# Two transformer layers after an attention stage: where ScalarE writes the scaled and shifted layer norm input, between the squares and the copies of transposed weights

## The reference

```python
x = layernorm(x + split_attention(dynamic_conv(x)))          # x: 16 x 256 x 128, "stage a"
x = layernorm(x + two_layers(x))

def layer(x):                                                # twice, 8 heads of 64
    h = shift_token(x)
    q, k, v = split(h @ wqkv)
    q, k = rotary_xpos(l2norm(q) * qs, l2norm(k) * ksc)
    o = local_attention(q, k, v)                             # windows of 64, softmax over 128 keys
    x = x + o @ wo
    h = shift_token(x)
    h = (h - mean(h)) / sqrt(var(h) + 1e-5) * ln_g + ln_b
    a, g = split(h @ w1 + b1)                                # 341 columns each
    return x + (a * gelu(g)) @ w2 + b2
```

## Time and profile before

| | us |
|---|---|
| median of 3 runs (1402.93 to 1405.08) | 1403.01 |
| the profiled execution's own time | 1405.44 |
| its span, first to last instruction | 1403.6 |
| busy in it: PE | 1249.5 (89%) |
| busy: VectorE | 1231.8 (88%) |
| busy: ScalarE | 944.8 (67%) |
| busy: GpSimd | 943.0 (67%) |

### The profile page before, as it was taken

One profiled execution on the slowest core, in us unless ns is written; L12 is line 12 of the kernel. 1 busy time (PEld: TensorE's weight loads), 2 busy tenths in 40 slices (PEclk: granted clock), 3 DMA queues, 4 the chain that ended last, 5 costly groups with the idle time before them and its releaser, 6 DMA issues.

```text
span 1403.6 us, 36296 instructions
## 1 busy us (share of the span) xinstructions
PE 1249.5 (89%) x12288; PEld 977.4 (70%) x12288; DVE 1231.8 (88%) x2418; ACT 944.8 (67%) x1708; POOL 943.0 (67%) x915
## 2 busy tenths in 40 slices
PE   4799889898988988988788999999999999999986
PEld 3577667776767766766566777777777777677764
DVE  4899999999999999998488888988888888888873
ACT  3566565666665656664367888888888877778772
POOL 0734443444344334444799999999999999999971
PEclk9899999999999999998999999999999999999998
DMA  5000000000000000000111212111122122211110
GB/s 170 1 10 13 9 7 12 12 11 9 11 11 4 9 11 11 8 7 14 25 41 36 51 43 47 45 45 43 46 53 49 42 52 48 50 46 44 47 35 27
DMA packets 87052, 44.15 MB, mean 31 GB/s; under 512 B 43908, under 2 KB 80176, under 8 KB 86960
## 3 DMA queue, kind: packets, MB, share of 16 engines
q1 hardware_dynamic: 86960, 42.95, 12.3%
HBM read 19.86 MB, written 6.29 MB: 19 GB/s over the span
## 4 chain that ended last, share of the span: by engine, by line
DVE 36%; POOL 25%; issue 17%; PE 17%; SPq 2%; ACT 1%; DVEq 1%; POOLq 0%; DMA 0%; ACTq 0%
DVE sums L993 9%; POOL rnorm L660 9%; POOL kT L649 7%; DVE probs L1025 7%; DVE mx L1019 5%; POOL probs L710 3%; POOL kT L663 3%; PE bank L1399 2%; DVE xo L1054 2%; PE bank L1378 2%; PE bank L1360 2%; PE bank L1434 2%; SPq L476 1%; DVE conv L936 1%; PE bank L1462 1%
## 5 line engine op out<-in xcount | busy, mean ns | idle before, releaser
L625 POOL TENSOR_TENSOR probs<-probs,coef 128x1024 f32<-128x1024 f32 x128 | 239.6, 1903 | 201.2 <-DVE coef L985 201.2
L660 POOL TENSOR_TENSOR rnorm<-norm,halves 128x8 f32<-128x8 f32 x128 | 213.8, 1671 | 10.7
L785 ACT ACTIVATE probs<-probs 128x1024 f32<-128x1024 f32 x128 | 134.7, 1052 | 101.7 <-DVE probs L1025 101.2
L1280 PE MATMUL bank<-ident,probs 128*128 128x128 f32 x1024 | 143.1, 284 | 50.0 <-POOL probs L625 49.9
L772 ACT ACTIVATE wT<-bank 128x512 f32<-128x512 f32 x256 | 138.8, 596 | 63.6 <-PE bank L1280 62.4
L1019 DVE TENSOR_REDUCE mx<-bank 128x8 f32<-128x512 f32 x256 | 163.7, 680 | 14.7 <-PE bank L1293 13.3
L649 POOL TENSOR_TENSOR kT<-qT 128x512 f32<-128x512 f32 x128 | 163.8, 1280 | 8.4 <-DVE qT L1073 8.4
L1280 PEld LDWEIGHTS bank<-ident,probs 128*128 128x128 f32 x1024 | 115.4, 144 | 69.5 <-POOL probs L625 58.5
L1025 DVE TENSOR_TENSOR probs<-bank,mx 128x512 f32<-128x512 f32 x256 | 163.4, 679 | 0.0
L1293 PE MATMUL bank<-kT,qT 64*128 64x256 f32 x1024 | 154.7, 423 | 6.3 <-DVE probs L1025 6.3
L1319 PE MATMUL bank<-wT,v 128*64 128x128 f32 x2048 | 144.3, 284 | 11.0 <-DVE gate L931 6.2
(11 more groups left out here) (120 smaller groups left out, 3082.7 us busy)
## 6 DMA issues: line engine op xcount, KB each, us to landing
probs<-f_v SPq DMA_DIRECT2D x96, 128.0 KB, 2.3
res<-stage_x SPq DMA_DIRECT2D x48, 128.0 KB, 3.9
xn<-in_x SPq DMA_DIRECT2D x16, 128.0 KB, 2.2
xr<-in_x SPq DMA_DIRECT2D x16, 128.0 KB, 2.2
stage_x<-xo SPq DMA_DIRECT2D x32, 64.0 KB, 1.6
hn<-stage_x SPq DMA_DIRECT2D x32, 64.0 KB
mn<-mid SPq DMA_DIRECT2D x64, 32.0 KB
stage_x<-yo SPq DMA_DIRECT2D x16, 128.0 KB, 2.1
```

The lines of the kernel that those rows point to most:

```text
L625: nc.gpsimd.tensor_tensor(out=e[:, :, :, :], in0=e[:, :, :, :], in1=coef[r][:, 2, A_REP * ng:A_REP * (ng + 1), :].unsqueeze(3).broadcast_t ...
L660: nc.gpsimd.tensor_tensor(out=rnorm[:, at], in0=norm2[:, 1, at], in1=halves[:, 0:F_HEADS], op=ALU.pow).then_inc(rnorm_set, 1)
L785: nc.scalar.activation(e[:, :, :, :], e[:, :, :, :], ACT.Exp).then_inc(exp_done, 1)
L1280: ins = nc.tensor.transpose(banks[4 + hp][:, P * (2 * kb + hh):P * (2 * kb + hh + 1)], e[:, 2 * hh + hp, 2 * kb:2 * kb + 2, :], ident[:, :])
```

## The change

In each tile 0 step of the two layers ScalarE did `hidden_input` first, then the squares of the even block, then the two copies into `eT`, then the exponential. Now `hidden_input` stands behind the two copies and ahead of the exponential. Nothing is added or removed.

```diff
--- before.py
+++ after.py
@@ -876,9 +876,6 @@
                         late = n - F_ATT_LAG
                         if tile == 1 and prepares(turn, p, 2):
                             rounded(it, p + 2, turn)
-                        local = f_late(turn, s, "gates")
-                        if local is not None:
-                            hidden_input(it, local, layer_of(local))
                         if prepares(turn, p):
                             squares(4 * (unit + 1) + 2 * tile, 4 * (p + 1) + 2 * tile, 2 * tile, turn)
                         if f_exists(turn, s, F_ATT_LAG):
@@ -887,6 +884,9 @@
                                 wait(act, f_o_made, late)
                                 nc.scalar.activation(eT[:, 4 * k:4 * k + 4, :], banks[4 + k][:, :].rearrange("p (h q) -> p h q", h=4),
                                                      ACT.Copy).then_inc(eT_read, 1)
+                        local = f_late(turn, s, "gates")
+                        if local is not None:
+                            hidden_input(it, local, layer_of(local))
                         if f_exists(turn, s):
                             e = fE[s % F_RING]
                             act.wait_ge(f_sub, n + 1)
```

## The result

The changed kernel takes 1412.24 us (median of 4 runs, 1410.79 to 1413.52) against 1402.97 us for the kernel before in the same session (1402.14 to 1405.08). The ratio is 1.0064, with a 95% interval of 1.0048 to 1.0080: the change makes the kernel 9.3 us slower. 1412.0 was predicted.

What follows compares the result with a forecast made beforehand. Two rings of equal length, GpSimd's and PE with VectorE's, were taken to bound layer one. Layer one's 9.2 us less 0.4, layer two nothing, took the median from 1403.0 to 1411.8, said as 1412.0; range 1405.8 to 1415.5.

Steps and rivals of the forecast that it cites:

- L855's new place, and PE's wait: Layer one, tile 0: L855 ends at 1003.93, so PE's odd block loads 0.68 to 0.69 us later.
- The ring of 20.60 us: Layer one: PE and VectorE's chain from one `mT` to the next, at most about 0.1 us of slack against 20.68.
- Squares and copies gain nothing: ScalarE, tile 0: the squares could start 0.03 us earlier; the copies gain nothing, bounds 0 to 0.03 us.
- The exponential has cover: ScalarE, tile 0: it moves from 1003.37 to about 1003.84 at no cost, with 0.67 us of cover before VectorE's sum.
- GpSimd falls in behind: Layer one: VectorE's rotated blocks come late, so from the second unit on GpSimd waits too.
- Sum for layer one: A unit takes 21.29 us; 15 units take 319.35 us in place of 310.17, 9.2 us more, or 8.8 net.
- GpSimd's lead: Layer one: VectorE's rotation ends 1.15 us (tile 1) or 0.85 us (tile 0) before L649; swallows about 0.4 us once.
- Layer two: Odd block 0.61 us late, but units stay at 22.28 us; cost nothing, cover about 1.0 us a unit.
- GpSimd covers it: Rival: busy GpSimd sets the pace, so a delay on PE and ScalarE costs nothing; 1403.0 us, chance 0.11.
- Half covered: Rival: PE's 0.40 us of idleness a unit in layer one absorbs part of the delay; 1407.4 us, chance 0.11.
- Faster: Rival: PE's odd block does not wait, squares and copies come up to 0.14 us earlier; 1401.5 us, chance 0.05.
- Layer two as well: Rival: 15 further units in layer two pay 0.61 us each, 9.2 us; 1421 us, chance 0.04.

Runs made afterwards that it cites:

- GpSimd relieved: Kernel before, with GpSimd dividing four of eight heads in a step and not five, ScalarE one more: 1397.17 us, ratio 0.9963.
- the same three matmuls: Kernel before plus three extra 128x512 PE matmuls: ahead of tile 0's odd block 1412.16 us, or ahead of tile 1's v block 1403.60 us.

## Why the prediction was right, point by point

- **L855's new place, and PE's wait.** Right. L855 starts 2.62 us behind `mT` (2.65 predicted). The odd block loads 0.62 us later, and 0.68 to 0.69 was predicted: the way from the end of L855 to PE's load is 1011.75 - (1011.12 + 0.58) = 0.05 us and not the 0.10 of the earlier trace rows, the start is 0.03 us early, and L855 takes 0.58 and not 0.56 us.
- **The ring of 20.60 us.** Right, and it carried the forecast. 21.24 - 0.62 = 20.62, and with GpSimd relieved the old order runs at 20.59.
- **Squares and copies gain nothing.** Right (0.01 us).
- **The exponential has cover.** Right here: VectorE's sum of it starts at 1013.36 behind other work, as foreseen. But in the kernels in which PE does not wait for L855, the late exponential or late copies show a price of 0.11 to 0.15 us a unit through the copy of transposed q and k, a path that the prediction did not look at. In the changed kernel the odd block and all behind it come 0.62 us later, and the stretch shows no wait of PE for that copy; so that it costs nothing there is an outcome that I had not argued for.
- **GpSimd falls in behind.** Right in substance, partly wrong in place. I had it waiting ahead of L649 in tile 1, 0.6 us a unit. From the second unit on it waits at both places: ahead of tile 0's L649, 0.29 us in the unit shown, and ahead of tile 1's, 0.11 to 0.19 us. The view above counts 22 of these waits, 5.1 us.
- **Sum for layer one.** 318.53 - 310.17 = 8.4 us, against 9.2 predicted, or 8.8 with the 0.4 us that GpSimd's lead was to give back. That term was wrong: the lead was used up, but the units take 21.21 us from the first of the stretch on, so it made none of them shorter. GpSimd's lead does not lie on the ring that sets the pace. With the measured 0.62 us the sum is 15 x 21.22 = 318.3 us, against 318.53 found. The upper bound of 0.80 us a unit was not net of slack either: 0.79 - 0.08 is 0.71. What was given back came later, 0.65 us on the way into layer two: the lateness of `mT` against before is 1.5 us at the start of the stretch (1.15 of it from before the change acts), 9.8 at its end, 10.0 two units on and 9.35 where the second stretch begins.
- **Layer two.** Right: PE's waits for L710 shrink by what the wait for L855 adds, the unit takes 22.32 against 22.28 us, and the change there alone is not to be told from no change.
- **The total.** 1412.0 was said and 1412.24 measured. That it came out to 0.3 us is luck: a step of 9.0 us was forecast, the interval of the measured one reaches from 6.7 to 11.2 us, and the terms had errors of 1 us (the wait) and 0.4 us (the lead) that partly cancel. What was right is the mechanism and its size to within 1 us or so. The span of the profiled execution grew by 7.9 us, the median by 9.3. Single executions differ before the change acts at all: the first `mT` of the layers starts between 747.3 and 752.5 us in the twelve profiles. At the last full unit's `mT` (1358.28 against 1348.69) the changed kernel is 9.6 us late; the tail behind it took 53.22 us at a granted clock of 0.92, and 54.91 us at 0.91 before. The tail varies between executions with nothing changed in it: the second row is of the kernel with L855 ahead of the copies, 57.47 us at 0.84.

```profile
1358.28:1411.50 53.22, 33.57 (x302) 26.79 (x298) 26.89 (x81) 20.64 (x38) 18.45 (x28) 0.92 0.11 28
```

```profile
1349.13:1406.60 57.47, 37.89 (x302) 30.09 (x298) 26.91 (x81) 21.07 (x38) 18.52 (x28) 0.84 0.10 26
```

- **The rivals.** GpSimd covers it, with the rule of the Trainium skill ("Perfetto Trace Analysis", section "Identifying the Most-Contended Engine") beside it: fallen. GpSimd was busy for 96.5% of layer one and back to back, and 0.62 us put on PE still cost 0.56 us a unit. Half covered (1407.4) falls with the same number. Faster falls, since L855 ended at 1011.70, and PE could have loaded the odd block at 1008.50 + 2.63 = 1011.13. Layer two as well falls by the run with layer two alone.

## What to carry to other kernels

When one engine works back to back, look for a second ring (a chain of waits that leads back to its own start, one unit later) before you call a delay elsewhere free: take the stretch of the trace where units come fastest, and see how much shorter it is than the mean (0.1 us here, so 0.62 us of wait cost 0.56). A reader of a shared PSUM bank belongs in its engine's order by when the next writer of that bank wants it, not by when its own result is used; L855's result was needed late, its bank early. And weigh a wait by its place in the ring: the same three matmuls cost 9.9 us ahead of the scores that VectorE waits for, and next to nothing ahead of a wait that was there anyway.

## What the runs showed of the hardware that was not expected

VectorE's scale-and-shift instruction from SBUF to SBUF (`tensor_scalar`, 128x128, fp32) gets longer when it starts under a large elementwise GpSimd instruction. L1091 takes 334 ns in the median before (in the window shown) and up to 801 ns in the kernel with L855 behind the exponential. Two of them took 0.59 us elsewhere and 1.02 us where they started under L663 (128x512, from 1015.76 to 1016.80). L1134 goes from 340 to 1292 ns in the median.

How much longer follows from when GpSimd's instruction ends. Over the profiles of all twelve kernels, 81 L1091 took over 400 ns, and each of them ended 80 to 88 ns behind the end of the GpSimd instruction under which it had started. The same holds for all 47 L1134 over 400 ns (81 to 85 ns). So it looks like a wait for the other to end, and not like two instructions that slow each other down in proportion. The kernel before has such cases too, outside the units shown.

Three kinds of pairs show no effect. L660 of GpSimd (128x8), though it runs for 1.67 us, lengthens nothing: all 347 L1091 that started under it took 332 to 356 ns. VectorE's sums from SBUF are not touched: 673 of L1076 that started under L663 took 669 to 679 ns, and 677 of L1173 under L649 or L663 took 1198 to 1220 ns. Nor are its instructions that read PSUM, such as L1195 (674 to 683 ns under L649).

This fits what the Trainium skill says ("SBUF — State Buffer", section "A bandwidth-pool intuition that's wrong (but worth ruling out)"): GpSimd and a VectorE instruction that uses two ports can't run at the same time, and one fully blocks. That L1091 is of that kind is argued from these rows and not isolated by a run. L660 shows that not every GpSimd instruction blocks for as long as it runs. In any case some tenths of a microsecond of delay on PE can bring more on VectorE, by what it then runs beside.
